# The first microseconds of an attention and deformable-convolution kernel: semaphore opening, weight preparation and group statistics in another order

## The chip, the cores and the metric

The kernel runs on one core of one Trainium2 chip. The metric is the device time of one execution in microseconds (us). The core has five engines that run beside one another and meet only at semaphores: TensorE (PE, matrix products into PSUM), VectorE (DVE), ScalarE (ACT), GpSimd (POOL) and SyncE (SP, which here issues all transfers). A "q" behind an engine's name in the profile (SPq, POOLq) is its instruction queue.

## The reference

The input x has shape (4, 128, 64, 64): four images of 128 channels and 4096 pixels. Two layers follow one another.

```
# layer 0
h    = group_norm(x, 32 groups) * norm_w + norm_b     # statistics over 4 channels x 4096 pixels
qkv  = einsum('bchw,dc->bdhw', h, qkv_w) + qkv_b
attn = softmax(einsum('bcn,bcm->bnm', q, k) * 128**-0.5)
x1   = x + proj_w @ (attn applied to v) + proj_b
# layer 1
y    = relu(batchnorm(conv3x3(x1, w1)))
off  = conv3x3(y, w_off) + b_off                      # 18 offsets per pixel
z    = batchnorm(deform_conv(y, off, w2))             # bilinear samples at 9 taps
out  = relu(z + x1)
```

## The kernel before, in words

Every engine has an instruction stream of its own, written out in a block (`block.sync`, `block.gpsimd`, `block.scalar`, `block.vector`, `block.tensor`). Within a stream, order is program order; between streams only semaphores order anything. f32 operands of matrix products are split into a high and a low f16 part, and three products stand for one.

Layer 0 goes through the images, and in each through 32 query tiles of 128 rows with four key chunks of 1024. Each chunk is one step of a software pipeline: scores on PE, their maximum on DVE, the exponential on ACT, the low part on POOL, a transfer that transposes, the product with the values on PE. Group norm and q, k, v of the next image are worked in between. Layer 1 is a convolution, the offsets, the sampling and a second convolution, and then a last sum and ReLU over 16 pieces, whose x1 (the residual) SP loads while the last tiles of the sampling still run.

The change is in the head, before the first scores. There:

- SP (L270 to L275) issues the first part of the weights, the first image in four pieces of 1024 pixels, the constants, and the rest of the weights, and then waits for `s_open`.
- Most semaphores (the dictionary `s`, and those of `s_xo`, `s_xs`, `s_tr`) are raised by 64 (`OPEN`) at the start, so that a helper `after(engine, key, count)` can wait for counts that would be below zero in the first steps of a loop. POOL does it with one increment per semaphore (L386 to L389) and then raises `s_open` (L390). PE, DVE and ACT wait for `s_open` before anything else. POOL then clears some tiles (L391 to L394).
- PE multiplies the projection weights into the value weights and bias (L1140, L1141). DVE scales the q weights (L777), copies the product from PSUM (L779) and scales the q bias (L780); its helper `link` counts each of these steps in `s_set` and waits for it. ACT waits for two of the steps and writes the high part of all three weights (L559); DVE subtracts it to get the low part (L783), adds a bias (L784) and waits for both.
- Then DVE takes the statistics of the eight half-pieces of the image (`gn_stats`, L841; every second one waits for a piece's transfer), merges them per channel (`gn_channel`, L858 to L861), and PE averages over the groups with a matrix out of the constants (`group_means`, L1218). DVE forms the variance (`gn_group`, L867 to L871), POOL raises it to the power -0.5 (L397), DVE forms scale and shift per channel (`gn_affine`, L877 to L881), and POOL applies them to the eight half-pieces (L401). ACT and DVE split the result (L598, L892) and PE starts on q, k and v (L1134 to L1136 by the helper `three`), with ACT and DVE emptying PSUM (L604, L609, L903, L909).

Of the kernel before, what the change touches and what calls it, by code (L numbers as in the profile page):

```python
# [20 lines left out]
ALU = mybir.AluOpType  # L21
# [3 lines left out]
B, C, HH, WW = 4, 128, 64, 64  # L25
# [43 lines left out]
V_NW, V_NB, V_BQ, V_BK, V_BV, V_BP, V_G1, V_B1, V_G2, V_B2, V_BO = range(W_VEC, W_VEC + 11)  # L69
# [5 lines left out]
H_2 = 3 * C  # L75
# [6 lines left out]
K_LO = K_JC + TAPS * WC  # L82
# [13 lines left out]
def build(nc, x, weights, consts, out):  # L96
# [7 lines left out]
    with ctx:  # L104
        def sem(name):
            return ctx.enter_context(nc.semaphore(name))

        def sb_in(scope, name, shape, dt):
            return scope.enter_context(nc.sbuf_tensor(name, shape, dt))


        WF = sb_in(ctx, "weights_f32", [128, W_ALL], F32)
        WH = sb_in(ctx, "weights_hi", [128, H_ALL], F16)
        WL = sb_in(ctx, "weights_lo", [128, H_ALL], F16)
        CN = sb_in(ctx, "constants", [128, K_LO], F32)
        OW = sb_in(ctx, "offset_w", [128, 2, TAPS, 32], F16)
        SM = sb_in(ctx, "small", [128, 64], F32)
# [82 lines left out]
        PS = ctx.enter_context(nc.psum_tensor("psum", [128, 8, 512], F32))  # L200
# [6 lines left out]
        s_k = sem("constants_loaded")  # L207
        s_kl = sem("late_constants_loaded")
        s_zf = sem("zero_rows_stored")
        s_open = sem("opened")  # L210
        s_set = sem("setup_steps")
        s_wh = sem("weights_hi_ready")
        s_ws = sem("weights_ready")
        s_bp = sem("bias_product")
        s_pz = sem("pool_cleared")
# [29 lines left out]
        def after(eng, key, count):  # L245

            eng.wait_ge(s[key], count + OPEN)
# [12 lines left out]
        def vec(i):  # L260
            return WF[:, i:i + 1]
# [7 lines left out]
        def _(sp):  # L269
            sp.dma_start(WF[:, 0:W_A], weights[:, 0:W_A]).then_inc(s_w, 16)  # L270
            for i in range(4):
                sp.dma_start(XIN[:, 1024 * i:1024 * i + 1024], x[0, :, 1024 * i:1024 * i + 1024]).then_inc(s_xq[i], 16)
            sp.dma_start(CN[:, :], consts[:, 0:K_LO]).then_inc(s_k, 16)
            sp.dma_start(WF[:, W_A:W_ALL], weights[:, W_A:W_ALL]).then_inc(s_wb, 16)
            sp.wait_ge(s_open, 1)  # L275

# [106 lines left out]

        @block.gpsimd
        def _(po):
            for k in s:  # L386
                po.sem_inc(s[k], OPEN)
            for k in s_xo + s_xs + s_tr:
                po.sem_inc(k, OPEN)  # L389
            po.sem_inc(s_open, 1)  # L390
            po.memset(OW[:, :, :, :], 0.0).then_inc(s_pz, 1)  # L391
            po.memset(SM[:, 0:1], -0.5).then_inc(s_pz, 1)
            po.memset(SM[:, 1:2], 1.0).then_inc(s_pz, 1)
            po.memset(Vh[:, :, :, 128:129], 1.0).then_inc(s_pz, 1)  # L394
            po.wait_ge(s_pz, 4)
            after(po, "gn", 6)
# [157 lines left out]

        @block.scalar
        def _(act):
            act.wait_ge(s_open, 1)
            act.wait_ge(s_set, 2)
            act.activation(WH[:, 0:H_2], WF[:, 0:H_2], ACT.Copy).then_inc(s_wh, 1)  # L559

# [205 lines left out]
        def _(ve):  # L766
            step = [0]

            def link(ins):

                step[0] += 1
                ins.then_inc(s_set, 1)
                ve.wait_ge(s_set, step[0])

            ve.wait_ge(s_open, 1)
            ve.wait_ge(s_w, 16)
            link(ve.tensor_scalar(WF[:, 0:C], WF[:, 0:C], float(C) ** -0.5, None, ALU.mult))  # L777
            ve.wait_ge(s_bp, 2)
            link(ve.tensor_copy(WF[:, 2 * C:3 * C], PS[:, 6, 0:C]))  # L779
            link(ve.tensor_scalar(SM[:, 2:3], vec(V_BQ), float(C) ** -0.5, None, ALU.mult))  # L780
            low = CL[:, 0:K_SH - K_LO].rearrange("p (q k) -> p q k", q=GPI)
            ve.wait_ge(s_wh, 1)
            link(ve.tensor_tensor(WL[:, 0:H_2], WF[:, 0:H_2], WH[:, 0:H_2], ALU.subtract))  # L783
            ve.tensor_tensor(SM[:, 3:4], PS[:, 7, 0:1], vec(V_BP), ALU.add).then_inc(s_ws, 1)  # L784
            ve.wait_ge(s_ws, 1)

            def unit(b, t, par, j, scores, late2, late4, final, phase):
                U = b * CPI + t * CPT + j
# [48 lines left out]
            def gn_stats(b, c):  # L837

                if c % 2 == 0:
                    ve.wait_ge(s_xq[c // 2], 16)  # L840
                ins = ve.bn_stats(ST6[:, c, :], XIN[:, 512 * c:512 * c + 512])  # L841
                if c == NCH - 1:
                    ins.then_inc(s["gn"], 1)
# [7 lines left out]
            def gn_channel(b):  # L851
                if b:
                    after(ve, "gs", b * NCH)

                g0 = b * GN_STEPS
                if b == 0:
                    after(ve, "gn", 1)
                ve.tensor_copy(SM[:, 40:41], ST6[:, NCH - 1, 1:2])  # L858
                ve.bn_aggr(SM[:, 4:6], ST6[:, :, :].rearrange("p a b -> p (a b)")).then_inc(s["gn"], 1 if b == 0 else 2)
                after(ve, "gn", g0 + 2)  # L860
                ve.scalar_tensor_tensor(SM[:, 5:6], SM[:, 4:5], SM[:, 4:5], SM[:, 5:6], ALU.mult, ALU.add).then_inc(s["gn"], 1)  # L861

            def gn_group(b, gbank):

                g0 = b * GN_STEPS
                after(ve, "gp", b + 1)
                ve.tensor_copy(SM[:, 9:11], PS[:, gbank, 0:2]).then_inc(s["gn"], 1)  # L867
                after(ve, "gn", g0 + 4)
                ve.scalar_tensor_tensor(SM[:, 6:7], SM[:, 9:10], SM[:, 9:10], SM[:, 10:11], ALU.mult, ALU.subtract).then_inc(s["gn"], 1)
                after(ve, "gn", g0 + 5)  # L870
                ve.tensor_scalar(SM[:, 7:8], SM[:, 6:7], -1.0, EPS, ALU.mult, ALU.add).then_inc(s["gn"], 1)  # L871

            def gn_affine(b):

                g0 = b * GN_STEPS
                after(ve, "rs", b + 1)
                ve.tensor_tensor(SM[:, 16:17], SM[:, 8:9], vec(V_NW), ALU.mult).then_inc(s["gn"], 1)  # L877
                after(ve, "gn", g0 + 7)
                ve.tensor_tensor(SM[:, 17:18], SM[:, 9:10], SM[:, 16:17], ALU.mult).then_inc(s["gn"], 1)
                after(ve, "gn", g0 + 8)  # L880
                ve.tensor_tensor(SM[:, 18:19], vec(V_NB), SM[:, 17:18], ALU.subtract).then_inc(s["gn"], 1)  # L881
                after(ve, "gn", g0 + 9)
# [11 lines left out]
            for c in range(NCH):  # L894
                gn_stats(0, c)
            gn_channel(0)
            gn_group(0, 0)
            gn_affine(0)
            def qkv_lo(b, c, kind, bank):

                after(ve, "evh", order(b, c, kind) + 1)
                if kind == 2:
                    ve.tensor_tensor(Vl[:, b % 2, 4 * c:4 * c + 4, :], PS[:, bank, :].rearrange("p (m o) -> p m o", m=4),  # L903
                                     Vh[:, b % 2, 4 * c:4 * c + 4, 0:128], ALU.subtract).then_inc(s["evl"], 1)
                else:
                    hi, lo = ((Qh, Ql), (Kh, Kl))[kind]
                    sl = slice(512 * c, 512 * c + 512)
                    bias = SM[:, 2:3] if kind == 0 else vec(V_BK)
                    ve.scalar_tensor_tensor(lo[:, b % 2, sl], PS[:, bank, :], bias, hi[:, b % 2, sl],  # L909
                                            ALU.add, ALU.subtract).then_inc(s["evl"], 1)  # L910
# [220 lines left out]
        def _(pe):  # L1131
# [3 lines left out]
                pe.matmul(dst, lh, rl, start=False, stop=False)  # L1135
                return pe.matmul(dst, ll, rh, start=False, stop=stop)  # L1136

            pe.wait_ge(s_open, 1)
            pe.wait_ge(s_w, 16)
            pe.matmul(PS[:, 7, 0:1], WF[:, W_PROJ:W_PROJ + C], vec(V_BV), start=True, stop=True).then_inc(s_bp, 1)  # L1140
            pe.matmul(PS[:, 6, 0:C], WF[:, 2 * C:3 * C], WF[:, W_PROJ:W_PROJ + C], start=True, stop=True).then_inc(s_bp, 1)  # L1141
            pe.wait_ge(s_ws, 1)
            pe.wait_ge(s_k, 16)

            def scores_of(b, U, t, j):
# [70 lines left out]
            def group_means(b, bank):  # L1216
                after(pe, "gn", b * GN_STEPS + 3)
                pe.matmul(PS[:, bank, 0:2], CN[:, K_GRP:K_GRP + 128], SM[:, 4:6], start=True, stop=True).then_inc(s["gp"], 1)  # L1218
# [13 lines left out]
                last.then_inc(s["qkv"], 1)  # L1232

            group_means(0, 0)

            after(pe, "gn", 4)
            for u in range(len(FIRST)):
# [218 lines left out]
```

## Time and profile before

| | us |
|---|---|
| median of three runs | 2370.48 |
| lowest and highest run | 2368.9, 2371.01 |
| the profiled execution | 2370.24 |
| span of its profile | 2368.3 |
| PE busy in the span | 2260.2 |

The span begins with the first instruction that the profiler shows; the execution's own time is 1.94 us longer. All times in the views count from the span's start. In the timeline a line is one instruction, or a run of equal ones (x8), with its start and length, and in brackets how long its engine stood idle before it and what released it. A landing time is the time from the issue of a transfer to its last byte.

### The profile page before, as it was taken

What the parts mean: (1) busy time and instruction counts of PE and PEld (TensorE: products, weight loads), DVE (VectorE), ACT (ScalarE), POOL (GpSimd) and SP (SyncE); (2) the same over time, 40 slices, a digit from 0 to 9 for tenths busy, and PEclk for the clock granted to TensorE, in tenths of its full rate; (3) what the DMA queues carried; (4) which work ended last, traced back from release to release, by engine and by line L of the source; (5) the groups of instructions that cost most, each with busy time, mean ns of one, the idle gap of its engine ahead of it and who ended that gap; (6) DMA issues with size and microseconds to landing.
All of it is one profiled execution on the core that took longest, in us unless ns stands there. A gap on an engine that the chain in (4) does not pass through costs nothing.

```text
span 2368.3 us, 73191 instructions
## 1 busy us (share of the span) xinstructions
PE 2260.2 (95%) x26668; PEld 1823.8 (77%) x26668; DVE 1808.2 (76%) x3885; ACT 1801.6 (76%) x2968; POOL 1448.9 (61%) x1103
## 2 busy tenths in 40 slices
PE   5999999999999999999999999969898999999994
PEld 3677777777777777777777777758666999999994
DVE  6778877777877777887777777758676887887887
ACT  5788888888888888888888888823376777776776
POOL 4569656666655666665666666675224666666661
PEclk9999999999999999999999999989999999999997
DMA  3878888879998888898787777786034444333447
GB/s 93 190 173 167 177 181 161 176 179 169 180 187 150 179 176 171 179 165 154 167 178 176 175 175 176 178 248 203 16 82 125 140 121 128 113 121 104 131 127 289
DMA packets 1048760, 377.63 MB, mean 159 GB/s; under 512 B 975490, under 2 KB 1035523, under 8 KB 1040387
## 3 DMA queue, kind: packets, MB, share of 16 engines
q1 hardware_dynamic: 1048578, 375.35, 68.8%
q8 instruction: 97, 1.59, 0.3%
q14 instruction: 85, 0.69, 0.1%
HBM read 98.69 MB, written 41.68 MB: 59 GB/s over the span
## 4 chain that ended last, share of the span: by engine, by line
PE 53%; POOL 24%; issue 16%; DVE 4%; DMA 2%; ACT 1%; POOLq 1%; SPq 0%; DVEq 0%; ACTq 0%
POOL interp L524 12%; POOL probs_split L416 10%; PE psum L1134 9%; PE psum L1135 9%; PE psum L1136 9%; PE psum L1174 7%; PE psum L1176 7%; PE psum L1175 7%; PE psum L1290 2%; DMA probsT_dma<-probs_split 2%; PE psum L1160 2%; PE psum L1298 1%; POOL col_hats L515 1%; POOL row_hats L510 1%; DVE neg_max L793 1%
## 5 line engine op out<-in xcount | busy, mean ns | idle before, releaser
L416 POOL TENSOR_TENSOR probs_split<-probs,probs_split 128x896 f16<-128x896 f32 x512 | 967.3, 1889 | 523.6 <-ACT probs_split L588 523.5
L793 DVE TENSOR_REDUCE neg_max<-psum 128x1 f32<-128x1024 f32 x512 | 626.4, 1223 | 307.6 <-PE psum L1136 305.3
L585 ACT ACTIVATE probs<-psum,exp_bias 128x1024 f32<-128x1024 f32 x512 | 570.5, 1114 | 184.6 <-DVE exp_bias L795 183.7
L1174 PE MATMUL psum<-vT_hi,probsT_dma 128*128 128x129 f16 x3584 | 637.6, 221 | 9.6 <-DMA probsT_dma<-probs_split 9.5
L1176 PE MATMUL psum<-vT_hi,probsT_dma 128*128 128x129 f16 x3584 | 637.3, 219 | 0.0
L1175 PE MATMUL psum<-vT_lo,probsT_dma 128*128 128x128 f16 x3584 | 637.1, 218 | 0.0
L588 ACT ACTIVATE probs_split<-probs 128x896 f16<-128x896 f32 x512 | 486.6, 950 | 23.1 <-ACT probs L585 1.0
L524 POOL TENSOR_TENSOR interp<-row_hats,col_hats 128x360 f32<-128x360 f32 x384 | 295.6, 798 | 185.4 <-PE psum L1311 174.4
L1134 PE MATMUL psum<-k_hi,q_hi 128*128 128x512 f16 x1024 | 388.5, 379 | 4.5 <-DVE q_lo L909 2.5
L1135 PE MATMUL psum<-k_lo,q_hi 128*128 128x512 f16 x1024 | 388.6, 379 | 0.0
L1136 PE MATMUL psum<-k_hi,q_lo 128*128 128x512 f16 x1024 | 388.6, 379 | 0.0
L1174 PEld LDWEIGHTS psum<-vT_hi,probsT_dma 128*128 128x128 f16 x3584 | 347.5, 97 | 11.2 <-DMA probsT_dma<-probs_split 10.9
L1175 PEld LDWEIGHTS psum<-vT_lo,probsT_dma 128*128 128x128 f16 x3584 | 352.8, 98 | 0.0
L1176 PEld LDWEIGHTS psum<-vT_hi,probsT_dma 128*128 128x128 f16 x3584 | 345.0, 96 | 0.0
L730 ACT ACTIVATE sampled_hi<-psum 128x432 f16<-128x432 f32 (+1 forms) x384 | 181.3, 497 | 81.3 <-PE psum L1136 81.2
L1063 DVE TENSOR_TENSOR sampled_lo<-psum,sampled_hi 128x432 f16<-128x432 f32 (+1 forms) x384 | 206.3, 554 | 47.1 <-ACT sampled_hi L730 42.5
L1055 DVE TENSOR_TENSOR interpT_lo<-psum,interpT_hi 120x384 f16<-120x384 f32 x384 | 190.4, 551 | 48.4 <-ACT interpT_hi L721 47.7
L1134 PE MATMUL psum<-sampled_hi,weights_hi 128*128 128x128 f16 x1152 | 214.4, 220 | 0.6 <-DVE sampled_lo L1063 0.6
L1136 PE MATMUL psum<-sampled_hi,weights_lo 128*128 128x128 f16 x1152 | 213.0, 219 | 0.0
L1135 PE MATMUL psum<-sampled_lo,weights_hi 128*128 128x128 f16 x1152 | 212.7, 219 | 0.0
L1134 PE MATMUL psum<-interpT_hi,xt_windows 120*128 120x144 f16 x1024 | 208.6, 227 | 2.1 <-DMA xt_windows<-xt_scratch 1.8
L721 ACT ACTIVATE interpT_hi<-psum 120x384 f16<-120x384 f32 x384 | 161.2, 492 | 64.9 <-PE psum L1311 54.2
(189 smaller groups left out, 4912.6 us busy)
## 6 DMA issues: line engine op xcount, KB each, us to landing
xt_windows<-xt_scratch SPq DMA_DIRECT2D x192, 320.0 KB
xt_scratch<-zeros_f SPq DMA_DIRECT2D x28, 576.0 KB, 4.3
probsT_dma<-probs_split SPq DMA_TRANSPOSE x512, 3.5
x_residual<-x SPq DMA_DIRECT2D x128, 64.0 KB, 2.4
x_scratch<-x_out SPq DMA_DIRECT2D x128, 64.0 KB, 2.1
x_rows<-x_scratch SPq DMA_DIRECT2D x32, 256.0 KB, 3.4
xt_scratch<-xt_stage SPq DMA_DIRECT2D x128, 64.0 KB
x_image<-x SPq DMA_DIRECT2D x3, 2048.0 KB, 9.1
```

The source lines that it names most:

```text
L416: po.tensor_tensor(PH[j][:, 1, :], P[:, j, 0:128 * DT[j]], PH[j][:, 0, :], ALU.subtract).then_inc(s["pl"], 1)
L524: last = po.tensor_tensor(SS[:, g % 2, :, WR * TW * a:WR * TW * a + WR * TW].rearrange("p k (j x) -> p k j x", j=WR), HX[:, hb, g, :, :, N ...
L585: act.activation(P[:, j, :], sc, ACT.Exp, bias=NB[:, par, j:j + 1]).then_inc(s["exp"], 1)
L588: act.activation(PH[j][:, 0, :], P[:, j, 0:128 * DT[j]], ACT.Copy).then_inc(s["ph"], 1)
L793: ve.tensor_reduce(NM[:, par, j:j + 1], sc, AX.X, ALU.max, negate=True).then_inc(s["mx"], 1)
L1063: ve.tensor_tensor(lo, src, hi, ALU.subtract).then_inc(s["xl"], 1)
L1134: pe.matmul(dst, lh, rh, start=start, stop=False)
L1135: pe.matmul(dst, lh, rl, start=False, stop=False)
L1136: return pe.matmul(dst, ll, rh, start=False, stop=stop)
L1174: pe.matmul(dst, th, Vh[:, p, v, 0:129], start=n == 0, stop=False)
L1175: pe.matmul(dst[:, 0:128], th, Vl[:, p, v, :], start=False, stop=False)
L1176: last = pe.matmul(dst, tl, Vh[:, p, v, 0:129], start=False, stop=n == KT - 1)
```

## The change

SP issues the constants between the second and the third piece of the image instead of after the fourth. POOL clears the two columns of `SM` before the increments. PE, DVE and ACT no longer wait for `s_open`. On DVE the copy of the weight product and the scaling of the q bias stand behind `gn_channel`, and the low part of the weights with the bias sum behind `gn_group`; the statistics come directly behind L777. PE waits for the finished weights (`s_ws`) behind `group_means` and not ahead of it. ACT's instructions and their wait for two steps of `s_set` stay.

```diff
@@ block.sync
             for i in range(4):
+                if i == 2:
+                    sp.dma_start(CN[:, :], consts[:, 0:K_LO]).then_inc(s_k, 16)
                 sp.dma_start(XIN[:, 1024 * i:1024 * i + 1024], x[0, :, 1024 * i:1024 * i + 1024]).then_inc(s_xq[i], 16)
-            sp.dma_start(CN[:, :], consts[:, 0:K_LO]).then_inc(s_k, 16)
@@ block.gpsimd
+            po.memset(SM[:, 0:1], -0.5).then_inc(s_pz, 1)
+            po.memset(SM[:, 1:2], 1.0).then_inc(s_pz, 1)
             for k in s:
                 po.sem_inc(s[k], OPEN)
...
             po.memset(OW[:, :, :, :], 0.0).then_inc(s_pz, 1)
-            po.memset(SM[:, 0:1], -0.5).then_inc(s_pz, 1)
-            po.memset(SM[:, 1:2], 1.0).then_inc(s_pz, 1)
@@ block.scalar
-            act.wait_ge(s_open, 1)
             act.wait_ge(s_set, 2)
@@ block.vector
-            ve.wait_ge(s_open, 1)
             ve.wait_ge(s_w, 16)
             link(ve.tensor_scalar(WF[:, 0:C], WF[:, 0:C], float(C) ** -0.5, None, ALU.mult))
-            ve.wait_ge(s_bp, 2)
-            link(ve.tensor_copy(WF[:, 2 * C:3 * C], PS[:, 6, 0:C]))
-            link(ve.tensor_scalar(SM[:, 2:3], vec(V_BQ), float(C) ** -0.5, None, ALU.mult))
-            ve.wait_ge(s_wh, 1)
-            link(ve.tensor_tensor(WL[:, 0:H_2], WF[:, 0:H_2], WH[:, 0:H_2], ALU.subtract))
-            ve.tensor_tensor(SM[:, 3:4], PS[:, 7, 0:1], vec(V_BP), ALU.add).then_inc(s_ws, 1)
-            ve.wait_ge(s_ws, 1)
...
             gn_channel(0)
+            ve.wait_ge(s_bp, 2)
+            link(ve.tensor_copy(WF[:, 2 * C:3 * C], PS[:, 6, 0:C]))
+            link(ve.tensor_scalar(SM[:, 2:3], vec(V_BQ), float(C) ** -0.5, None, ALU.mult))
             gn_group(0, 0)
+            ve.wait_ge(s_wh, 1)
+            link(ve.tensor_tensor(WL[:, 0:H_2], WF[:, 0:H_2], WH[:, 0:H_2], ALU.subtract))
+            ve.tensor_tensor(SM[:, 3:4], PS[:, 7, 0:1], vec(V_BP), ALU.add).then_inc(s_ws, 1)
+            ve.wait_ge(s_ws, 1)
             gn_affine(0)
@@ block.tensor
-            pe.wait_ge(s_open, 1)
             pe.wait_ge(s_w, 16)
             pe.matmul(PS[:, 7, 0:1], ...).then_inc(s_bp, 1)
             pe.matmul(PS[:, 6, 0:C], ...).then_inc(s_bp, 1)
-            pe.wait_ge(s_ws, 1)
             pe.wait_ge(s_k, 16)
...
             group_means(0, 0)
+            pe.wait_ge(s_ws, 1)
```

## Rows read from the trace of the kernel before

**Rows 1.** The page, busy time of each engine, its share and instructions.

```profile
PE 2260.2 (95%) x26668; PEld 1823.8 (77%) x26668; DVE 1808.2 (76%) x3885; ACT 1801.6 (76%) x2968; POOL 1448.9 (61%) x1103
```

**Rows 2.** Chain that ended last, first 7 us, shares by line.

```profile
by line: issue 72.5%; POOLq L387 16.0%; PE psum L1140 5.3%; POOLq L389 1.9%; POOLq L390 0.4%; POOLq L1450 0.2%
```

**Rows 3.** Waits, first 35 us: total us, times, longest.

```profile
DVE weights_f L777 <- POOLq L390: 6.9, 1, 6.9
```

**Rows 4.** Timeline of DVE, 0 to 21 us: start, length, instruction.

```profile
8.27 0.29 DVE L779 COPY weights_f<-psum 128x128 f32<-128x128 f32 x1 [1.12 <-PE psum L1141]
...
10.56 0.56 DVE L783 TENSOR_TENSOR weights_lo<-weights_f,weights_hi 128x384 f16<-128x384 f32 x1 [1.81 <-ACT weights_hi L559]
11.15 0.16 DVE L784 TENSOR_TENSOR small<-psum,weights_f 128x1 f32<-128x1 f32 x1
11.35 4.84 DVE L841 BATCH_NORM_STATS2 gn_stats<-x_image 128x6 f32<-128x512 f32 x8
16.23 0.15 DVE L858 COPY small<-gn_stats 128x1 f32<-128x1 f32 x1
...
16.69 0.22 DVE L861 SCALAR_TENSOR_TENSOR small<-small 128x1 f32<-128x1 f32 x1
17.65 0.16 DVE L867 COPY small<-psum 128x2 f32<-128x2 f32 x1 [0.74 <-PE psum L1218]
...
18.10 0.15 DVE L871 TENSOR_SCALAR small<-small 128x1 f32<-128x1 f32 x1
18.99 0.16 DVE L877 TENSOR_TENSOR small<-small,weights_f 128x1 f32<-128x1 f32 x1 [0.73 <-POOL small L397]
...
19.38 0.16 DVE L881 TENSOR_TENSOR small<-weights_f,small 128x1 f32<-128x1 f32 x1
```

**Rows 5.** Timelines of the other engines, same stretch.

```profile
8.64 1.28 ACT L559 ACT_TABLE_LOAD   x1 [8.64 <-DVE weights_f L779]
9.94 0.52 ACT L559 ACTIVATE weights_hi<-weights_f 128x384 f16<-128x384 f32 x1
...
7.39 0.77 PE L1141 MATMUL psum<-weights_f 128*128 128x128 f32 x2
17.06 0.56 PE L1218 MATMUL psum<-small,constants 128*128 128x2 f32 x2 [8.89 <-DVE small L861]
...
6.99 0.67 POOL L391 MEMSET offset_w<- 128x576 f16 x1 [6.53 <-issue]
...
18.41 0.55 POOL L397 TENSOR_TENSOR small<-small 128x1 f32<-128x1 f32 x1 [10.36 <-DVE small L871]
```

**Rows 6.** Timeline of SP, 0 to 9 us: the issues.

```profile
1.21 1.84 SPq L272 DMA_DIRECT2D x_image<-x  x4
3.09 0.62 SPq L273 DMA_DIRECT2D constants<-consts  x1
```

**Rows 7.** Issues at 0.76, 1.21, 2.14, 2.62 and 3.09 us: KB, us to landing.

```profile
weights_f<-weights SPq DMA_DIRECT2D x1, 261.5 KB, 2.7
...
x_image<-x SPq DMA_DIRECT2D x1, 512.0 KB, 4.3
...
x_image<-x SPq DMA_DIRECT2D x1, 512.0 KB, 7.1
...
x_image<-x SPq DMA_DIRECT2D x1, 512.0 KB, 7.9
...
constants<-consts SPq DMA_DIRECT2D x1, 227.0 KB, 8.1
```

**Rows 8.** Timeline, 0 to 45 us: two matmuls of 512 columns on PE.

```profile
24.56 0.63 PE L1134 MATMUL psum<-h_hi,weights_hi 128*128 128x512 f16 x1
...
27.96 0.38 PE L1134 MATMUL psum<-h_hi,weights_hi 128*128 128x512 f16 x1
```

**Rows 9.** Two stretches: length, busy time of PE, PEld, DVE, ACT, POOL, granted clock, DMA.

```profile
68.00:71.50 3.50, 0.81 (x14) 0.64 (x13) 1.63 (x3) 2.12 (x4) 1.61 (x1) 1.00 1.27 238
71.80:75.20 3.40, 3.40 (x17) 1.74 (x15) 0.97 (x2) 0.06 (x1) 1.89 (x1) 0.51 1.51 196
```

## The prediction, made before the changed kernel was run

> **What bounds the kernel now.** I read the page first. PE is busy 95% of the span [rows 1], so beyond the head the kernel is a pipeline fed by PE; nothing in the edit touches it. What the edit can change is when that pipeline starts, and the size of any gain is capped by the head.
>
> The head is read in the chain of waits. Up to 7 us nearly all of it is POOL raising semaphores: "issue" and POOLq L387 to L390 [rows 2]. DVE's first instruction stood 6.9 us for POOL's L390 [rows 3], although its weights, issued at 0.76, had landed 2.7 us later, at 3.46 [rows 7]. From there the timeline of DVE is to be read beside those of ACT and PE. The weights are prepared first: copy at 8.27, then 2.0 us of idle and other work until L783 at 10.56, because ACT loads its function table (1.28) and writes the high part (0.52) in between [rows 4, 5]. Only at 11.35 do the eight statistics start; they take 4.88 us to the copy at 16.23 [rows 4]. By 11.35 nearly all of the image is there: its pieces are issued at 1.21, about 1.67, 2.14 and 2.62, and the first, third and fourth land at 5.5, 9.24 and 10.52, the constants at 11.19 [rows 6, 7]. From 16.23 on, the chain is L861, the group means on PE, L867 to L871, the power on POOL, and `gn_affine` at 18.99 [rows 4, 5]. All that follows hangs on `gn_affine`: POOL, ACT, DVE and PE touch h only behind it. So I measure the change by the time at which L877 starts, now 18.99.
>
> **The change part by part.**
>
> *No wait for the opening.* DVE starts at about 3.5 (weights at 3.46) instead of 6.92, and PE's two products start there too and are done by about 4.9. POOL's opening still ends near 7.0 (its two memsets, 0.1 us each or less, now stand ahead of the increments). The first instruction that needs an opened semaphore is the copy of `gn_channel` (L858), which comes after 12 below, so the opening is hidden with 5 us to spare. ACT's missing wait is worth nothing by itself: it waits for `s_set` anyway. SP still waits for the opening, with nothing to issue before some 50 us.
>
> *Statistics first.* They are now bound by the transfers. Eight take 4.88, so one more adds 0.60 and the last 0.68 [rows 4]. The first two run from 5.5, the next two as the second piece lands, near 8.
>
> *Constants ahead of the third piece.* This is another 227 KB in front of pieces three and four, and 0.62 instead of nothing on SP's queue. The queue isn't empty then (piece three lands 7.1 us after its issue), so what counts is the bytes: the constants landed 0.67 us behind the fourth piece [rows 6, 7], and I push both pieces by that: 9.9 and 11.19. From below the price is 0 (piece four at 10.52; then the last four statistics, running from 9.9 without a gap, end 2.5 us later at 12.4), from above twice 0.67 (11.86). I take 11.19. In return the constants come at about 8.6, which nobody needs: their reader, L1218, starts at 13.3 or later. The move costs what it costs and buys nothing here; the rest of the weights is issued last in both and its readers on POOL come behind L401.
>
> Then: fourth piece at 11.19, some 0.06 to wake DVE, 0.60 + 0.68 for the last two statistics: L858 at 12.53 instead of 16.23. L861 follows 0.46 later as now, at 12.99 [rows 4]. Up to here 3.70 us are gained.
>
> *Weight preparation behind the statistics.* L779 and L780 now stand directly behind L861. L779 starts at about 13.23 and takes 0.29; both lie in the 0.74 us for which DVE waits for PE now [rows 4], so L867 is not late: 13.95, and L871 ends at 14.55. But L779 is also what ACT waits for, and ACT's chain isn't shortened by anything. It runs as now [rows 4, 5]: 0.08 after the end of L779 the table load (13.60), 1.30 later the activation (14.90), 0.62 later L783 on DVE. That is 15.52. DVE has stood idle from 14.55, and `gn_affine` is queued behind L783 in program order. POOL's power, which runs from 14.71 to 15.26, is done meanwhile; it is no longer what ends the wait. L783 to L784 takes 0.59, L784 to the next instruction 0.20: L877 starts at 16.31.
>
> The new wait thus gives back 1.02 us of the 3.70 (16.31 against 15.29, which is 18.99 - 3.70); 2.68 are left. For each end: if the table load stood before the wait, at the start of ACT's stream, the activation would come at 13.60 and L783 would follow L871 at once, at about 14.6: L877 at 15.39, a gain of 3.60. From the other side, the bound is that L779 is held up by something until PE's product: L867 then goes with it, and each tenth counts once; I allow 0.3. I take 2.68: the table load of the kernel before sat idle until L779 had ended, though ACT had nothing else to do [rows 5], so it stands behind the wait and the wait is unchanged.
>
> On the table load a page and the trace differ. The activation starts 0.02 us after the load has ended [rows 5]. The Trainium skill, "ScalarE: Activation LUTs", What ACT_TABLE_LOAD costs, gives about 1283 ns for the load, which this row has, and about 1380 ns more for a drain, 2.66 us for every switch. Now that the load is on the path, the sum would be a gain of 2.68 by the row and of 1.30 by the page's figure, an estimate; I give that 3 in 100.
>
> *Behind L877* nothing changes: L401, the splits and q, k, v are the same instructions in the same order, and they wait for one another only. PE's wait for `s_ws` is met before it needs h. All later transfers are issued when computed data is ready, so they move along. There is no clock time in the program that could absorb the 2.68 us.
>
> **The sum.** Profiled execution: 2370.24 - 2.68 = 2367.56, its span 2365.6. The median of the runs is 0.24 above the profiled one, so the forecast for the median is 2367.8.
>
> **The rivals.**
>
> 1. *The table load goes to the front* (above): L877 at 15.39, 2370.48 - 3.60 = 2366.9. For it: one wait fewer ahead of it. Against: it did not pass the other wait before. 8 in 100.
>
> 2. *The gain is swallowed.* This would need a later wait that ends at a fixed time. The only long idle time of PE near the start is 2.7 us at 68 to 70.9, where PE was busy 0.81 of 3.5 us while the DMA engines were full [rows 9]. Its transfers are issued by waits on computed data, so it should move along; if the burst of transfers there ended no earlier, the time stays 2370.5. 7 in 100.
>
> 3. *Slower: more stretches at the lower clock.* After that idle time PE was granted 0.51 of its clock (the 1.2 GHz level instead of 2.4) for 3.4 us, in which it was busy throughout [rows 9]. Such a stretch costs up to 1.7 us of work. If the shifted start makes it longer or calls up new ones, the change loses from 2.68 / 0.5 = 5.4 us more at the lower level on; three more such stretches cost 5.1 and give 2370.48 - 2.68 + 5.1 = 2372.9. For it: the stretch follows an idle time, and how the two lie to each other may shift. Against: the runs of before differ by 2.1 us at most. 7 in 100 that it is at least this, and the same thing the other way, a stretch or two fewer, 2366.1 or 2364.4, 6 in 100. In the head PE is slow too: 512 columns took 0.63 us at 24.56 and 0.38 at 27.96 [rows 8]; DVE and POOL set the pace there, so a clock that rises as late as now costs little.
> The Trainium skill, "TensorE: Matmul & The Clock Gate", The HAM clock gate, says of this that the number of slow matmuls at a start changes from run to run of one kernel; no single trace can show that, and it would put a us or so on either side.
>
> 4. *The change does not do what it says*, a start of the statistics held by something else (the instruction stream, the first piece landing late): L841's last two are bound by the last piece, so a late start costs nothing until it is over 4 us late. 2 in 100.
>
> **How the numbers follow.** The likeliest case, a gain of 1.9 to 3.2 us (2367.3 to 2368.6), has 70 in 100 with the 3 of the drain beside it. With the spread of the runs (about 1 us each way) and rivals 1 and 2, the range 2365.0 to 2371.3 leaves some 15 in 100 out. A measurement of this kernel tells 0.2% (4.7 us) from no change. Faster by more, under 2365.7, needs stretches of low clock to vanish or rival 1 with a good run: 9 in 100. Slower by more, over 2375.2, needs 14.8 us more at the lower level: 4 in 100. The rest, 87 in 100, is within.
>
> **What would show it.** In the trace of after: L777 at 3.5; the last L841 starts at about 11.9 and L858 at 12.5; the table load directly behind L779 at 13.6; DVE idle about 1.0 us before L783, released by ACT; L877 at 16.3; PE's first L1134 at 19.4 (22.05 - 2.68) and everything up to 60 us earlier by the same. The prediction is wrong if L877 is not within 15.3 to 16.8, or if the shift of 2.7 us seen there isn't found again at the end.

## The result, and the profile after

The changed kernel took 2365.31 us (median of 20 runs), the kernel before 2369.42 (median of 20 runs beside them): a ratio of 0.9984, with a 95% interval of 0.9977 to 0.9990, that is 3.8 us less (2.4 to 5.4). The forecast was 2.7 us less and 2367.8; 1.1 us of the distance to 2365.31 is the kernel before itself, whose median was 2370.48 in the three runs that the forecast started from. The profiled execution took 2364.74 us, its span is 2362.9.

The timeline of DVE after the change answers to [rows 4] (line numbers have moved: the statistics are L833, the copy behind them L850, the weight copy L890, the low part of the weights L894, the first step of `gn_affine` L869):

```profile
3.47 0.23 DVE L776 TENSOR_SCALAR weights_f<-weights_f 128x128 f32<-128x128 f32 x1 [3.47 <-DMA weights_f<-weights]
5.35 2.52 DVE L833 BATCH_NORM_STATS2 gn_stats<-x_image 128x6 f32<-128x512 f32 x4 [1.66 <-DMA x_image<-x]
8.54 1.29 DVE L833 BATCH_NORM_STATS2 gn_stats<-x_image 128x6 f32<-128x512 f32 x2 [0.67 <-DMA x_image<-x]
10.12 1.29 DVE L833 BATCH_NORM_STATS2 gn_stats<-x_image 128x6 f32<-128x512 f32 x2 [0.30 <-DMA x_image<-x]
11.44 0.15 DVE L850 COPY small<-gn_stats 128x1 f32<-128x1 f32 x1
...
11.91 0.22 DVE L853 SCALAR_TENSOR_TENSOR small<-small 128x1 f32<-128x1 f32 x1
12.05 0.29 DVE L890 COPY weights_f<-psum 128x128 f32<-128x128 f32 x1
...
12.95 0.16 DVE L859 COPY small<-psum 128x2 f32<-128x2 f32 x1 [0.42 <-PE psum L1215]
...
13.39 0.15 DVE L863 TENSOR_SCALAR small<-small 128x1 f32<-128x1 f32 x1
13.46 0.55 DVE L894 TENSOR_TENSOR weights_lo<-weights_f,weights_hi 128x384 f16<-128x384 f32 x1
...
14.53 0.16 DVE L869 TENSOR_TENSOR small<-small,weights_f 128x1 f32<-128x1 f32 x1 [0.32 <-POOL small L398]
```

The start of the statistics is released by a transfer and not by POOL's queue, and so is the pair behind each later gap. `gn_affine` starts at 14.53 instead of 18.99: 4.46 us earlier, where 2.68 were forecast. 1.09 of the 1.78 between them is the fourth piece, which landed at 10.10 and not at the forecast 11.19. The timelines of ACT, POOL and PE, to be read beside [rows 5], have the next reason in their first line:

```profile
0.75 1.28 ACT L559 ACT_TABLE_LOAD   x1 [0.75 <-PEq L1448]
12.37 0.52 ACT L559 ACTIVATE weights_hi<-weights_f 128x384 f16<-128x384 f32 x1 [10.33 <-DVE weights_f L890]
...
13.70 0.72 POOL L398 TENSOR_TENSOR small<-small 128x1 f32<-128x1 f32 x1 [5.76 <-DVE small L863]
...
17.57 0.59 PE L1133 MATMUL psum<-h_hi,weights_hi 128*128 128x512 f16 x1 [4.74 <-DVE h_lo L884]
```

The table load has gone to 0.75 us, the start of ACT's stream, so the activation follows the weight copy at once and the low part of the weights (13.46) waits for nothing. PE's first product of q, k, v starts at 17.57; before it was at 22.05. That start is what I compare from here on, and call the lead of a kernel.

How far that lead goes can be read at one kind of instruction whose first and last start are given. First before, then after; the first values of the attention:

```profile
L820 DVE TENSOR_SCALAR values_sum<-psum,chunk_factor x128: 341/351/355, 57.1 to 1541.6; 128x129 f32<-128x129 f32 x128
```
```profile
L812 DVE TENSOR_SCALAR values_sum<-psum,chunk_factor x128: 341/350/355, 54.2 to 1536.2; 128x129 f32<-128x129 f32 x128
```

At the first start (57.1) the lead is 2.9 and at the last (1541.6) it is 5.4, the difference of the spans. The stretches tell why. In the columns of [rows 9], after:

```profile
38.90:42.30 3.40, 3.40 (x10) 1.17 (x9) 1.38 (x2) 0.28 (x1) 0.00 (x0) 0.50 0.00 0
71.80:75.20 3.40, 3.40 (x39) 2.48 (x37) 2.65 (x8) 2.53 (x4) 0.88 (x1) 1.00 1.00 214
```

and the first of them before:

```profile
38.90:42.30 3.40, 1.76 (x18) 0.96 (x15) 3.40 (x7) 1.95 (x3) 0.00 (x0) 1.00 0.02 5
```

After the change PE is granted half its clock (1.2 GHz) at 38.9 to 42.3, where it had the full one before, and has the full one at 71.8 to 75.2, where before it had half [rows 9]. The first costs 1.6 us of the lead (4.5 to 2.9). The second gives 1.9 back, as the same maximum behind it shows, before and then after, 4.8 apart:

```profile
83.73 1.22 DVE L793 TENSOR_REDUCE neg_max<-psum 128x1 f32<-128x1024 f32 x1 [0.64 <-PE psum L1136]
```
```profile
78.98 1.23 DVE L785 TENSOR_REDUCE neg_max<-psum 128x1 f32<-128x1024 f32 x1 [0.63 <-PE psum L1135]
```

The last 0.6 gathers in steps of up to 0.4, one of them backwards, up to 900 us; their causes stay open. So of the 5.4 us between the two profiled executions the head made 4.5.

### The profile page after: what moved, and what is told of

The parts are those of the page before. It is cut to its first block, busy times and chain, and to the rows that moved or that the text cites. A ratio compares the mean times of both kernels' runs of the same rounds, so it can differ in the third digit from the quotient of the medians.

```text
span 2362.9 us, 73188 instructions
## 1 busy us (share of the span) xinstructions
PE 2260.3 (96%) x26668; PEld 1824.9 (77%) x26668; DVE 1807.0 (76%) x3885; ACT 1800.0 (76%) x2968; POOL 1448.8 (61%) x1103
## 4 chain that ended last, share of the span: by engine, by line
PE 54%; POOL 24%; issue 15%; DVE 3%; DMA 2%; ACT 1%; POOLq 1%; SPq 0%; DVEq 0%; ACTq 0%
POOL interp L525 12%; POOL probs_split L417 10%; PE psum L1133 9%; PE psum L1135 9%; PE psum L1134 9%; PE psum L1171 7%; PE psum L1173 7%; PE psum L1172 7%; PE psum L1288 2%; DMA probsT_dma<-probs_split 2%; PE psum L1157 2%; PE psum L1296 1%; PE psum L1278 1%; POOL col_hats L516 1%; POOL row_hats L511 1%
```

## The experiments

"Ratio" is that of a kernel's runs to the runs of the kernel before on the same chip, with its 95% interval. "Two waits on ACT", "constants last", "512 KB more" and "before again" have one execution each, the profiled one, so only their heads are compared.

**Two waits on ACT.** The step that failed was the place of the table load. The trace of before had a row for it: the second of ACT's two waits (L558) was an instruction of its own, and the load stood behind it.

```profile
L558 ACTq EVENT_SEMAPHORE  x1: 17/17/17, 8.6 to 8.6; - x1
```

After the change there is no such row.

```diff
         def _(act):
+            act.wait_ge(s_open, 1)
             act.wait_ge(s_set, 2)
```

> The changed kernel with one edit: ACT again waits for the opening ahead of its wait for two steps of s_set. My theory: what freed the function table load (0.75 us in the changed kernel, 8.64 before) is that only one wait stands ahead of the activation, which then carries it, so the load has nothing ahead of it; with two, the second is an instruction of its own ahead of the load. Then the load starts about 0.08 after the copy of the product has ended, at 12.4, the activation at 13.7, the low part of the weights at 14.3 and gn_affine at 15.1 instead of 14.53: 0.6 us later, with DVE idle about 0.8 before the low part. Rival A: the load stays at 0.75 and nothing moves (14.5), then its place has to do with something else in the edit. Rival B: the load goes between the two waits and starts at 7.0, again 14.5.

ACT and then DVE in its timelines:

```profile
13.61 1.28 ACT L560 ACT_TABLE_LOAD   x1 [13.61 <-DVE weights_f L891]
14.90 0.52 ACT L560 ACTIVATE weights_hi<-weights_f 128x384 f16<-128x384 f32 x1
...
14.58 0.15 DVE L864 TENSOR_SCALAR small<-small 128x1 f32<-128x1 f32 x1
15.45 0.56 DVE L895 TENSOR_TENSOR weights_lo<-weights_f,weights_hi 128x384 f16<-128x384 f32 x1 [0.72 <-ACT weights_hi L560]
...
16.24 0.16 DVE L870 TENSOR_TENSOR small<-small,weights_f 128x1 f32<-128x1 f32 x1
```

The load is back behind the weight copy, and DVE idles 0.72 us for it, as the theory has it; rivals A and B are out. From L864 to `gn_affine` it is 1.66 us and 1.14 in the changed kernel, so the free load is worth 0.52. The absolute 16.24 is later than the 15.1 expected because the fourth piece landed at 11.29 in this execution and at 10.10 in the other. All profiles agree on the place: with one wait ahead of the activation (eight profiles) the load starts at 0.75 or 0.76, with two (the kernel before twice, this one, the order alone) behind the weight copy, at 8.64, 8.64, 13.61 and 13.29. The activation starts 0.01 us behind the load here too: no drain, now with the load on the path.

**The waits for the opening alone.**

```diff
         def _(act):
-            act.wait_ge(s_open, 1)
             act.wait_ge(s_set, 2)
...
-            ve.wait_ge(s_open, 1)
             ve.wait_ge(s_w, 16)
...
-            pe.wait_ge(s_open, 1)
             pe.wait_ge(s_w, 16)
```

> The kernel before with only the three waits for the opening taken out; order of the work and of the transfers as before. My theory: the statistics end 1.3 us after the last piece has landed whichever stands first, because the weight preparation fits into the time before the pieces land. Weights scaled at 3.5, copy of the product at 4.9, low part at 5.8, statistics from 6.6 without a gap to about 11.5, or 1.3 after the last piece (landing at 9.5 to 10.5), so gn_affine starts at 13.6 to 14.6 against 14.53 in the changed kernel and 18.99 before, and the time is that of the changed kernel, 0.998 of before. Rival: the order is what counts and each part has a share of its own; then only the 3.45 us of the missing wait are gained, gn_affine at 15.5, ratio 0.9985, and the changed kernel stays 1 us ahead.

```profile
5.79 0.56 DVE L781 TENSOR_TENSOR weights_lo<-weights_f,weights_hi 128x384 f16<-128x384 f32 x1 [0.47 <-ACT weights_hi L558]
...
6.58 4.98 DVE L839 BATCH_NORM_STATS2 gn_stats<-x_image 128x6 f32<-128x512 f32 x8
11.60 0.15 DVE L856 COPY small<-gn_stats 128x1 f32<-128x1 f32 x1
...
14.36 0.16 DVE L875 TENSOR_TENSOR small<-small,weights_f 128x1 f32<-128x1 f32 x1 [0.73 <-POOL small L397]
```

`gn_affine` at 14.36 and a ratio of 0.9980 (0.9971 to 0.9989): the old order of the work without the waits has the whole gain. The rival's 15.5 is out. Reordering DVE and moving the constants added nothing to it that these runs can tell.

**The order alone.**

```diff
+            act.wait_ge(s_open, 1)
             act.wait_ge(s_set, 2)
...
+            ve.wait_ge(s_open, 1)
             ve.wait_ge(s_w, 16)
...
+            pe.wait_ge(s_open, 1)
             pe.wait_ge(s_w, 16)
# and the constants issued behind the fourth piece
```

> The changed kernel with the waits for the opening back on PE, ACT and DVE and the constants in their old place, so only the order of the work is changed. My theory: statistics from 7.3 without a gap for 4.88, their end at 12.1; the copy of the product at 12.7; ACT has two waits, so the table load is behind the copy (13.1), the activation at 14.4, the low part at 15.0, gn_affine at 15.8: 3.2 us of the 4.46 are there with the opening waited for, ratio 0.9986. Together with the kernel that only drops the waits this shows that the two halves of the change replace one another. Rival: without the early start the order brings no more than the 1.9 us of waiting for ACT's activation that it covers, gn_affine at 17, ratio 0.9992.

```profile
7.24 5.04 DVE L834 BATCH_NORM_STATS2 gn_stats<-x_image 128x6 f32<-128x512 f32 x8
...
15.14 0.56 DVE L895 TENSOR_TENSOR weights_lo<-weights_f,weights_hi 128x384 f16<-128x384 f32 x1 [0.72 <-ACT weights_hi L559]
...
15.93 0.16 DVE L870 TENSOR_TENSOR small<-small,weights_f 128x1 f32<-128x1 f32 x1
```

`gn_affine` at 15.93, 3.06 us earlier than before, ratio 0.9986 (0.9976 to 0.9997), as expected. One half alone gives 4.6 us in the head, the other 3.1, both 4.5 or, below, 3.1: they replace one another, because each brings the end of the statistics to the landing of the last piece. The order alone has the table load on its path too (13.29), with two waits on ACT, which is about 0.5 us of its distance.

**The place of the constants.**

```diff
-                if i == 2:
-                    sp.dma_start(CN[:, :], consts[:, 0:K_LO]).then_inc(s_k, 16)
                 sp.dma_start(XIN[:, 1024 * i:1024 * i + 1024], ...)
+            sp.dma_start(CN[:, :], consts[:, 0:K_LO]).then_inc(s_k, 16)
```

> The changed kernel with the constants issued behind the fourth piece again. My theory (a step of the prediction): the move costs the third and fourth piece the time of 227 KB, about 0.6 us, and brings nothing; without it they land at about 7.9 and 9.5 instead of 8.52 and 10.10, the copy behind the statistics starts at 10.8 instead of 11.44 and gn_affine at 13.9 instead of 14.53. Constants at 10.1, before the group means at 11.7 need them. Rival: the order of issue does not matter because the sixteen engines take the transfers side by side; the fourth piece lands at 10.1 as before and gn_affine stays at 14.5. A second rival: the constants, now last, hold the group means back, and the gain is lost there.

```profile
10.96 1.29 DVE L832 BATCH_NORM_STATS2 gn_stats<-x_image 128x6 f32<-128x512 f32 x2 [0.63 <-DMA x_image<-x]
...
15.36 0.16 DVE L868 TENSOR_TENSOR small<-small,weights_f 128x1 f32<-128x1 f32 x1 [0.32 <-POOL small L397]
```

This missed: the fourth piece landed at 10.93 and not at 9.5, and `gn_affine` came 0.8 us later than in the changed kernel. The second piece, which both kernels issue ahead of the constants, had landed at 7.78 here and at 6.57 there, so more than that distance was there before the order could matter. And with more in front of the third piece:

```diff
                 if i == 2:
                     sp.dma_start(CN[:, :], consts[:, 0:K_LO]).then_inc(s_k, 16)
+                    sp.dma_start(WF[:, W_A:W_A + 1024], weights[:, W_A:W_A + 1024]).then_inc(s_wb, 16)
...
-            sp.dma_start(WF[:, W_A:W_ALL], weights[:, W_A:W_ALL]).then_inc(s_wb, 16)
+            sp.dma_start(WF[:, W_A + 1024:W_ALL], weights[:, W_A + 1024:W_ALL]).then_inc(s_wb, 16)
...
-            po.wait_ge(s_wb, 16)
+            po.wait_ge(s_wb, 32)
```

> The changed kernel with 512 KB of the late weights issued behind the constants and before the third piece, so that 739 KB and not 227 stand there. It enlarges the suspected cost of that place. My theory: the time of the bytes is added, 512 KB at about 0.38 MB/us are 1.3 us, so the third piece lands at about 10.0 and the fourth at 11.5, and gn_affine comes at about 15.9. Rival: the engines take the transfers side by side, the fourth piece stays at 10.1 to 11.3 as in the five kernels so far.

```profile
10.80 2.59 DVE L834 BATCH_NORM_STATS2 gn_stats<-x_image 128x6 f32<-128x512 f32 x4 [2.00 <-DMA x_image<-x]
...
16.50 0.16 DVE L870 TENSOR_TENSOR small<-small,weights_f 128x1 f32<-128x1 f32 x1 [0.32 <-POOL small L399]
```

The third piece landed at 10.78 and the fourth at 12.08. Whether that is the bytes or chance takes all profiles. This is where the pieces land (issue and time to landing) in each execution of this study that issues weights first. The second piece is issued ahead of the constants in all of them:

| kernel | second piece lands at | third, us behind the second | fourth, us behind the second | fourth lands at |
|---|---|---|---|---|
| *constants behind the fourth* | | | | |
| before | 7.97 | 1.30 | 2.57 | 10.54 |
| before again | 7.42 | 1.29 | 2.53 | 9.95 |
| opening alone | 7.78 | 1.25 | 2.47 | 10.25 |
| order alone | 7.81 | 1.26 | 3.17 | 10.98 |
| constants last | 7.78 | 1.24 | 3.16 | 10.93 |
| *constants ahead of the third* | | | | |
| changed | 6.57 | 1.95 | 3.53 | 10.10 |
| changed again | 7.95 | 1.90 | 3.57 | 11.52 |
| two waits | 7.73 | 1.84 | 3.56 | 11.29 |
| statistics six times | 8.31 | 1.85 | 3.72 | 12.03 |
| *constants and 512 KB ahead of the third* | 7.49 | 3.29 | 4.59 | 12.08 |

The last column alone settles nothing: the same order scatters by 1.0 to 1.9 us from one execution to the next, more than the 0.67 us in question, and the means (10.53 and 11.24) differ by 0.71 with a standard error of about 0.45. But much of this scatter is already in the second piece, ahead of which nothing was moved. Counted from there, the third piece comes 1.24 to 1.30 us later in the one order and 1.84 to 1.95 in the other, the fourth 2.47 to 3.17 and 3.53 to 3.72, without overlap. The constants themselves land 0.58 to 0.60 behind the second piece. So the move costs about 0.6 us at the third piece and 0.8 at the fourth, about what the prediction said (0.67), and the 512 KB cost 1.4 and 1.0 more in their one profile (1.3 expected). The rival, by which the order of issue does not matter, is out. That the move gains nothing is shown by the group means, which start behind L853 and never for the constants.

**Does the lead reach the end?**

```diff
+            for k in range(5):
+                for c in range(NCH):
+                    if c % 2 == 0:
+                        ve.wait_ge(s_xq[c // 2], 16)
+                    at = 12 * (8 * k + c)
+                    ve.bn_stats(HNh[:, at:at + 12].bitcast(F32), XIN[:, 512 * c:512 * c + 512])
             for c in range(NCH):
                 gn_stats(0, c)
```

> The changed kernel in which DVE takes the statistics of the eight half-pieces five more times into a scratch tile before the real ones: 40 more instructions of 0.60 us in a row, about 24.2 us on the path of the head. My theory: what the head gains or loses reaches the end one for one, since nothing later waits for a fixed time. Then gn_affine starts about 24 us later and the time is 24 us longer: some 2389.5, ratio to before 1.0085 (0.998 and 24.2 / 2369). Rival: the pipeline absorbs a part of such a shift, so that also of the 4.46 us of the head only a part is real and the rest of the 4.1 is chance; then the time grows by clearly less, 15 us or under.

```profile
40.18 0.16 DVE L869 TENSOR_TENSOR small<-small,weights_f 128x1 f32<-128x1 f32 x1 [0.32 <-POOL small L398]
```

`gn_affine` is 21.2 us later than in the kernel before in this profile, and 25.7 later than in the first profile of the changed kernel, 1.9 of that because the fourth piece landed at 12.03. The ratio is 1.0076 (1.0062 to 1.0091), or 18.0 us (14.7 to 21.6), with the expected 1.0085 and the 21.2 inside the interval. The growth over the changed kernel is 18.0 and 3.8, or 21.8, with some 3.8 either way, so the rival's 15 or less is out. With the others:

| kernel | lead at PE's first product, us | time less by, us (interval) |
|---|---|---|
| changed | 4.5 | 3.8 (2.4 to 5.4) |
| changed, second profile and runs | 3.1 | 3.3 (0.7 to 5.9) |
| opening alone | 4.6 | 4.7 (2.6 to 6.9) |
| order alone | 3.1 | 3.3 (0.7 to 5.7) |
| statistics six times | -21.2 | -18.0 (-21.6 to -14.7) |
| image first (below) | 5.9 | 7.1 (4.3 to 9.7) |
| image first, second | 6.1 | 5.4 (3.1 to 7.8) |

In each row the lead lies in the interval of the time. The six gains add up to 27.3 us in the heads and to 27.6 in the times, while of the 21.2 us of delay 18.0 were measured (0.69 to 1.02 of it). So the head's lead reaches the end about one for one, and a loss of a few tenths of it on the way is not excluded.

**The kernels before and after once more.**

> The kernel before, unchanged, for a second profile. My theory: the head comes out as before with gn_affine at 19.0, since the last piece lands long ahead of its use there, while the landings scatter by a us and the stretches at the lower clock in the first 80 us lie elsewhere. Rival: the landings and stretches of low clock are properties of the kernel, and come out as in the first profile (fourth piece at 10.54, one stretch at 71.8).

In it `gn_affine` started at 18.99 again, although the fourth piece had landed 0.6 us earlier (9.95), and in two stretches PE had the lower clock, neither of them at 71.8:

```profile
43.40:46.70 3.30, 3.30 (x9) 1.12 (x8) 1.38 (x2) 0.16 (x1) 0.00 (x0) 0.50 0.00 0
74.10:77.40 3.30, 3.30 (x15) 1.71 (x13) 1.66 (x3) 0.28 (x1) 1.53 (x1) 0.50 1.31 162
```

The first values of the attention start at 58.6 in this profile and at 57.1 in the first one, though the heads are equal:

```profile
L820 DVE TENSOR_SCALAR values_sum<-psum,chunk_factor x128: 339/350/355, 58.6 to 1543.2; 128x129 f32<-128x129 f32 x128
```

So the stretch at 43.4 alone costs about 1.6 us, in one and the same kernel.

> The changed kernel unchanged, for a second profile, on the same chip as the version with the image first. My theory: in the head the fourth piece lands between 10 and 11.5, and gn_affine follows its landing by 4.4 us (14.4 to 15.9); against the kernel before the gain is what the head gained, 3 to 4.5 us, ratio 0.9981 to 0.9987. The stretches at the lower clock before 80 us lie at other places than 38.9. Rival: the first profile (fourth piece at 10.10, one stretch at 38.9) repeats itself and the ratio is 0.998.

```profile
11.54 1.29 DVE L833 BATCH_NORM_STATS2 gn_stats<-x_image 128x6 f32<-128x512 f32 x2 [0.39 <-DMA x_image<-x]
...
15.94 0.16 DVE L869 TENSOR_TENSOR small<-small,weights_f 128x1 f32<-128x1 f32 x1 [0.32 <-POOL small L398]
```

The lead of the changed kernel is 3.1 us here and 4.5 in its first profile, with nothing but the landing between them; the ratio was 0.9986 (0.9975 to 0.9997). Its lower clock fell at 40.4 and 71.1.

**A version that follows the chain.** If the last landing sets the head, the image must come first, its last piece must be small, and nothing may stand between the power and `gn_affine`.

```diff
-            sp.dma_start(WF[:, 0:W_A], weights[:, 0:W_A]).then_inc(s_w, 16)
-            for i in range(4):
...
+            for i, (at, n) in enumerate(PIECES):    # (0, 1024), (1024, 1024), (2048, 1024), (3072, 512), (3584, 512)
+                sp.dma_start(XIN[:, at:at + n], x[0, :, at:at + n]).then_inc(s_xq[i], 16)
+            sp.dma_start(CN[:, :], consts[:, 0:K_LO]).then_inc(s_k, 16)
+            sp.dma_start(WF[:, 0:W_A], weights[:, 0:W_A]).then_inc(s_w, 16)
# DVE: statistics, gn_channel, scale of the q weights, gn_group, gn_affine,
#      then weight copy, q bias, low part of the weights, bias sum
# PE:  group_means, then the two bias products, then the wait for s_ws
```

> A version that follows the chain: the image is issued first, in pieces of 1024, 1024, 1024, 512 and 512 pixels, then the constants, then the first part of the weights; gn_affine comes before all preparation of the weights but the scaling of the q part, and the bias products stand behind the group means on PE. No engine but SP waits for the opening. My theory: the end of the statistics is the last piece's landing and 0.7 us (one half-piece and not two), and the landing is earlier by the 261 KB of weights and 227 KB of constants, so it comes at 9 to 9.5, the statistics end at 9.9, the group means run at 10.7, gn_affine at 12.4 and PE's first product of q, k, v at 15.5 against 17.57: 2 us less than the changed kernel, 2363.3, ratio 0.9972. Rival: the weights, landing last at 10.5 or later, take the place of the image: PE runs the bias products at 11 to 12.3, ACT's activation follows at 12.9, the low part at 13.6, and if any of it is 1.5 us later than that, PE's first product waits for the weights and nothing is gained.

```profile
4.90 5.11 DVE L832 BATCH_NORM_STATS2 gn_stats<-x_image 128x6 f32<-128x512 f32 x8 [4.90 <-DMA x_image<-x]
...
12.88 0.16 DVE L868 TENSOR_TENSOR small<-small,weights_f 128x1 f32<-128x1 f32 x1 [0.73 <-POOL small L399]
...
14.41 0.56 DVE L896 TENSOR_TENSOR weights_lo<-weights_f,weights_hi 128x384 f16<-128x384 f32 x1 [0.47 <-ACT weights_hi L560]
...
16.12 0.58 PE L1134 MATMUL psum<-h_hi,weights_hi 128*128 128x512 f16 x1 [3.63 <-DVE h_lo L883]
```

Ratio 0.9970 (0.9959 to 0.9982), PE's first product at 16.12 and not at 15.5. The statistics now run with hardly a gap from 4.90 (5.1 us for eight, 4.84 in [rows 4]), while the last piece has landed at 8.83, so the last landing no longer sets their end; DVE nearly does. Of the miss of 0.6 us, 0.1 is their end (10.04), 0.3 my sum for the chain from there to `gn_affine` (2.84 and not 2.5), and 0.2 the low part of the weights, which holds back the first `h_lo`.

> The version with the image first and gn_affine ahead of the weights again, beside the changed kernel on one chip. My theory: PE's first product of q, k, v at 16.1 as in its first profile, 1.5 to 3 us ahead of the changed kernel, and the time lower by that, ratio 0.9972 to before. Rival: its first ratio of 0.997 had 2 us of chance in it and it does not differ from the changed kernel (both 0.998).

0.9977 (0.9967 to 0.9987), 2363.81 us beside 2364.55 of the changed kernel on the same chip; first product at 15.93. It is faster than the kernel before in both comparisons; against the changed kernel the trace shows 1.5 to 3.1 us in the head, but the intervals of the times overlap, so that in the whole time this is not shown.

## Why the prediction was right, and where not

The direction, the size and "within 0.2%" came out, and so did the range. But the gain of 3.8 us lies above the likeliest case (1.9 to 3.2), and the median of 2365.31 is only 0.3 us inside the range and below the prediction's own mark for "faster by more" (2365.7). Against the kernel before in the runs beside it, whose median is 1.1 us lower than that of the three at hand, the change is within 0.2%. The 20 runs of before lie 6.9 us apart, where the prediction counted on 2.1. By its own test for the head (L877 between 15.3 and 16.8) the prediction was wrong in the first profile, 14.53, and in the second it is inside, 15.94, with a late landing in place of the table load. Step by step:

- *No wait for the opening; statistics first.* Right: L776 (L777 before) at 3.47 (3.5 forecast), the first statistics at 5.35 (5.5), L850 1.34 us behind the fourth landing (1.34 forecast). What it did not say is that either half alone would do: by [rows 4, 7] the opening alone would have shown the same end of the statistics, and I did not make that sum.
- *"It stands behind the wait and the wait is unchanged".* This step of the likeliest case failed, and rival 1, with 8 in 100, was what happened. The argument was that the load had not passed a wait before. But the kernel before had two waits there, and only the second was an instruction; the change took the first, the remaining one rides on the activation, and the load has nothing ahead of it. Two waits on ACT in the changed kernel brought it back. Its price was 0.52 us, not the 0.92 of the rival's sum (3.60 - 2.68).
- *Fourth piece at 11.19.* The price of the constants in it (0.67) was right, by the table of the landings. What was off was the start: the second piece landed at 6.57 where the kernel before had 7.97, and at 7.95 in the next profile of the same changed kernel. That is chance, so the fourth landed at 10.10 in the one and at 11.52 in the other. The first gives 1.09 us of the 1.78 by which the head did better than the forecast, the table load 0.52, and 0.17 are left over. The kernel with two waits shows the same remainder: its weight copy (L891) starts 0.14 behind L854 (0.24 forecast), and its low part (L895) 0.55 behind the activation (0.62).
- *Power on POOL hidden.* With the load out of the way POOL ends the wait again: DVE stands 0.32 us for L398. The rival's sum had DVE end it, with `gn_affine` 2.40 us behind L861; in the changed kernel it is 2.62. The likeliest case's sum had 3.32 and the kernel with two waits has 3.14. These 0.22 and 0.18 are the 0.40 by which the rival's price was off.
- *Nothing later absorbs it.* Right within the intervals of the table of leads.
- *Rival 3.* The stretches at the lower clock did move, both ways at once, and do so in executions of one and the same kernel. Each is worth 1.6 to 1.9 us of a single execution, so two single profiles can't be compared to better than that. In the first 80 us the kernel before had one and two of them in its two profiles, and the changed kernel one and two; that they have a part in the change's gain is not shown.
- *The drain.* The figure of the Trainium skill ("ScalarE: Activation LUTs", What ACT_TABLE_LOAD costs) did not come up: the activation followed the load by 0.01 us also where the load was on the path (13.61 + 1.28, then 14.90).

What stays open: why the second piece lands at 6.6 us in one execution and at 7.4 to 8.3 in the others, and whether the version with the image first is faster than the changed kernel in the whole time.

## What to carry to other kernels

Where two changes each bring a stage to the same floor (here the landing of the last piece), work out each alone: the sum of their gains isn't there, and one of them is enough. Look in the trace for a wait's own instruction in front of a table load; in all profiles here a single wait rode on the activation, and the load then stood at the front. And in a head of 20 us, a landing time from one profile is good to a us, no better: what an order of issue costs is read from the distance of two landings in the same profile, the first of them of a transfer issued ahead of what was moved.

## What the runs showed of the hardware

- POOL's power of a 128x1 column took 0.72 us in the five profiles in which DVE's 128x384 subtraction into f16 ran beside it (changed, changed again, constants last, 512 KB more, statistics six times), and 0.55 in the seven others (before twice, two waits, opening alone, order alone, image first twice).
- The same six transfers (weights, constants and four pieces), issued at the same times, had all landed at 10.1 to 12.0 us from one execution to the next.
- 227 KB issued ahead of two other transfers on the same queue moved the landing of the next one by 0.6 us (1.27 to 1.88 us behind the second piece, means of five and four profiles).
- POOL's 75 increments of semaphores took from 0.7 to 6.9 us, most of them 0.08 us apart (before).
- The one table load of each kernel took 1.28 us, and the activation followed it by 0.02 us or less wherever the load was waited for (before twice, two waits, order alone).
- The stretches of 3.4 us at the lower clock (0.50 granted) lay in other places in each execution: at 71.8 and at 43.4 and 74.1 in the kernel before, at 38.9 and at 40.4 and 71.1 in the changed one, and in the first of the two image-first profiles none was granted between 20 and 1500 us.
